# One norm for two, a rounding step without GpSimd, and sixteen gather places in a four-layer transformer kernel

## What is computed

```python
def _layernorm(x, axis=-1, eps=1e-05):
    return (x - mean(x)) / jnp.sqrt(var(x) + eps)

# third attention: it is called with _layernorm(x), and norms its input once more
def _L2_xattn_ref(hidden_states, cond, ln_w, ln_b, ...):
    ln_out = _ln(hidden_states, ln_w, ln_b)          # the second norm in a row
    # _fp8_linear_pertensor(ln_out, w, w_scale, in_scale), for q, k, v and qx:
    #   y = clip(ln_out / in_scale, -448, 448) -> bfloat16 -> float8_e4m3fn
    ...

# fourth feed-forward part: 64 experts, the best 8 for each token, 128 places an expert
def _L3_ffn_ref(hidden_states, router_weight, gate_up_proj, down_proj):
    topw, topi = jax.lax.top_k(softmax(x @ router_weight.T), 8)
    xe = x gathered by expert                        # (64, 128, 256)
    h = silu(g) * u                                  # g, u = xe @ gate_up_proj
    ye = h @ down_proj                               # (64, 128, 256)
    y = sum over the 8 experts of ye[its place] * weight

x = x + _L2_xattn_ref(_layernorm(x), ctx, ...)
...
x = x + _L3_ffn_ref(_layernorm(x), ...)
```

## Time and profile before

| | |
|---|---|
| Runs | 1892.12, 1887.36, 1890.64 us; median 1890.64 |
| Profiled execution | 1887.24 us, span of its instructions 1885.5 us |
| Mean granted TensorE clock | 0.871 of full speed |
| Busy (share of the span) | TensorE 1544.3 us (82%), VectorE 1120.1 (59%), ScalarE 813.7 (43%), GpSimd 777.2 (41%) |
| First norm to the end of the rounding stage | 868.2 to 921.8 us |
| Gathers and scatters of the sparse stage | 1678.6 to 1853.8 us |

### The profile page before, as it was taken

How to read it: one execution, slowest core, us unless ns; L and a number is a source line. 1 busy time by engine, 2 the same in 40 slices (tenths; PEclk the granted TensorE clock), 3 DMA queues, 4 the chain that set the end, 5 groups by cost and what they waited for, 6 DMA issues and landing times. The chain is left out here.

```text
span 1885.5 us, 25460 instructions
## 1 busy us (share of the span) xinstructions
PE 1544.3 (82%) x8600; PEld 982.3 (52%) x8600; DVE 1120.1 (59%) x2581; ACT 813.7 (43%) x1887; POOL 777.2 (41%) x1038
## 2 busy tenths in 40 slices
PE   6566659999797899994499999999699989837772
PEld 5322225656464455653266676666556565525551
DVE  5999971223674533426789999999622255463335
ACT  2898863110333211113488888888521112412221
POOL 1276641000200497800578777777310000026772
PEclk9666558999697999997699999999799988858886
DMA  2298871110504013111100000000111100146646
GB/s 76 59 180 180 177 153 44 34 42 17 179 2 163 34 56 120 56 45 46 45 1 1 2 1 1 1 2 1 43 29 39 37 24 1 69 177 214 244 140 239
DMA packets 174225, 140.13 MB, mean 74 GB/s; under 512 B 141793, under 2 KB 154721, under 8 KB 170386
## 3 DMA queue, kind: packets, MB, share of 16 engines
q1 hardware_dynamic: 165314, 114.89, 21.4%
q0 software_dynamic: 6416, 22.03, 3.5%
q10 hardware_dynamic: 2368, 1.61, 0.3%
HBM read 85.43 MB, written 19.50 MB: 56 GB/s over the span
## 5 line engine op out<-in xcount | busy, mean ns | idle before, releaser
L1817 POOL CAST l0m_pi<-l0m_pf 128x1024 bf16<-128x1024 int16 x128 | 133.2, 1040 | 111.1 <-ACT l0m_pf L1884 109.6
L1420 PE MATMUL l2x_pr<-l_w,l2x_xq 128*128 128x512 bf16 x576 | 141.4, 384 | 40.0 <-ACT credits L42 40.0
L350 PE MATMUL l1e_gu<-x_normT,l1e_w 128*128 128x512 f32 x384 | 171.6, 601 | 0.0
L1884 ACT ACTIVATE l0m_pf<-l0m_s,l0m_bias,l0x_sq 128x1024 int16<-128x1024 f32 x128 | 153.9, 1204 | 18.7 <-DVE l0m_bias L1915 12.3
L1911 DVE TENSOR_REDUCE l0m_mx<-l0m_s 128x1 f32<-128x1024 f32 x128 | 155.5, 1215 | 5.5 <-PE l0m_s L1826 5.2
L1555 DVE TENSOR_SCALAR l2x_raw<-l2x_raw,l2x_mv,l2x_rs 128x128 f32<-128x128 f32 x384 | 141.7, 429 | 1.6 <-POOL l2x_rs L1399 1.5
L1826 PE MATMUL l0m_s<-l0x_kT,l0x_qT 64*128 64x512 bf16 x256 | 69.0, 559 | 68.5 <-ACT l0m_pf L1884 65.7
L350 PE MATMUL l0e_gu<-x_normT,l0e_w 128*128 128x512 f32 x272 | 121.2, 600 | 0.0
L350 PEld LDWEIGHTS l1e_gu<-x_normT,l1e_w 128*128 128x128 f32 x384 | 74.0, 194 | 84.3 <-issue 83.3
L350 PE MATMUL l2e_gu<-x_normT,l2e_w 128*128 128x512 f32 x256 | 114.5, 602 | 0.0
L426 DVE TENSOR_TENSOR l1e_h<-l1e_sil,l1e_gu 128x512 f32<-128x512 f32 x40 | 27.5, 686 | 133.0 <-ACT l1e_sil L402 133.0
(11 more groups left out here) (516 smaller groups left out, 3562.8 us busy)
## 6 DMA issues: line engine op xcount, KB each, us to landing
l3m_w<-in_l_moe SPq DMA_DIRECT2D x16, 1280.0 KB, 6.4
l1e_w<-in_l_ffn SPq DMA_DIRECT2D x24, 384.0 KB, 3.0
l_rows<-zero_row SPq DMA_DIRECT2D x8, 1024.0 KB, 11.0
l_w<-l_rows SPq DMA_DIRECT2D x8, 1024.0 KB, 11.8
l0e_w<-in_l_ffn SPq DMA_DIRECT2D x17, 384.0 KB, 3.0
l2e_w<-in_l_ffn SPq DMA_DIRECT2D x16, 384.0 KB, 3.1
ctx_tok<-l_route SPq DMA_DIRECT2D x8, 512.0 KB
l2q_wps<-in_l_wp SPq DMA_DIRECT2D x16, 256.0 KB, 2.8
```

Source lines behind the costliest of these rows:

```text
L350: last = nc.tensor.matmul(gu[half][:, m, :], w[:, c % SW, (2 * k + m) * P:(2 * k + m + 1) * P], pg.xnT[:, k, cols(n)], start=(k == 0), sto ...
L1420: last = nc.tensor.matmul(flat(pr[t % 2][:]), src[:, k, tokens], pg.l2_w3[:, part, k, at:at + W], start=(k == 0 and part == 0), stop=(k == ...
L1817: nc.gpsimd.tensor_copy(pi[:, n % 8, :], pf[:, n % 4, :]).then_inc(s["rounded"], 1)
L1884: nc.scalar.activation(pf[:, n % 4, :], s_ps[n % 3][:], ACT.Exp, scale=sq[:, b, h:h + 1], bias=bias[:, n % 4:n % 4 + 1], accum_out=sm[:, b ...
```

## The change

Three things. The two norms in a row become one: the first norm is turned and takes the square root of var(1 + eps) + eps^2, which is what two norms in a row divide by; the block `l2xm` and the option `turn` go. The subtraction of the rounding stage moves from GpSimd to VectorE, as a fifth instruction of each job. The sparse stage has sixteen places for gathered rows, of which eight are filled ahead of the first scatter and two more behind each scatter until sixteen are reached; they lie in the buffer of the third layer's weights, which is no longer needed then, in place of a buffer of their own.

```diff
-def norm(pg, name, src, preload=None, turn=True):
+def norm(pg, name, src, preload=None, twice=False):
...
-                v.tensor_scalar(rs[:, 0, group], mv[:, group, 1], LN_EPS, None, ALU.add).then_inc(var_in, 1)
+                if twice:
+                    v.tensor_scalar(rs[:, 0, group], mv[:, group, 1], 1.0 + LN_EPS, LN_EPS ** 2, ALU.mult, ALU.add).then_inc(var_in, 1)
+                else:
+                    v.tensor_scalar(rs[:, 0, group], mv[:, group, 1], LN_EPS, None, ALU.add).then_inc(var_in, 1)
...
-            for i in range(PAIRS if turn else 0):
+            for i in range(PAIRS):
...
-    norm(pg, "l2xm", pg.xn)
...
-            @block.gpsimd
-            def _(pool):
-                for n, (k, j) in enumerate(jobs):
-                    pool.wait_ge(widened, n + 1)
-                    nc.gpsimd.tensor_tensor(xq[:, j, k, :], wide[:, n % 2], step[:, n % 2], ALU.subtract).then_inc(rounded, 1)
...
                     dve.wait_ge(divided, n + 1)
-                    if n >= 2:
-                        dve.wait_ge(rounded, n - 1)
                     ch.link(nc.vector.tensor_scalar(z[:, u], z[:, u], 448.0, -448.0, ALU.min, ALU.max))
                     widen(nc, ch, z[:, u], step[:, u], wide[:, u]).then_inc(widened, 1)
+                    dve.wait_ge(widened, n + 1)
+                    nc.vector.tensor_tensor(xq[:, j, k, :], wide[:, u], step[:, u], ALU.subtract).then_inc(rounded, 1)
+                dve.wait_ge(rounded, len(jobs))
...
-    GROUP, LOADS, AHEAD, NY = 4, 6, 6, 4
+    GROUP, LOADS, AHEAD, FIRST, NY = 4, 6, 16, 8, 4
...
-        xg = sb("xg", [P, AHEAD, ROW])
...
+        xg = spent[:, 0:AHEAD * ROW].rearrange("p (a n) -> p a n", n=ROW)
...
-            for e in range(AHEAD):
+            for e in range(FIRST):
                 gather(e)
             pool.wait_ge(pg.rows_zeroed, 16 * 8)
             for e in range(E):
                 scatter(e)
-                if e + AHEAD < E:
-                    gather(e + AHEAD)
+                for n in range(min(FIRST + 2 * e, e + AHEAD), min(FIRST + 2 * e + 2, e + AHEAD + 1)):
+                    if n < E:
+                        gather(n)
...
-                norm(pg, f"{name}n", pg.x, pre.load if pre else None, name != "l2x")
+                norm(pg, f"{name}n", pg.x, pre.load if pre else None, name == "l2x")
```

More of the change, by code:

```diff
@@ L195, in _ @@
         def _(pe):
-            if not turn:
-                return
             for i in range(PAIRS):
```

## The result

The changed kernel took 1862.9 us (median of 4 runs, 1858.9 to 1864.57), the kernel before on the same chip 1889.19 (4 runs, 1887.36 to 1892.12): ratio 0.9856, 95% interval 0.9833 to 0.9879. The profiled execution took 1861.34 us with a span of 1859.6, against 1885.5.

The account below looks back on a forecast made before the run. No single engine was taken to bound the kernel: VectorE stretched by GpSimd set rounding, GpSimd's issuing the sparse stage. Gains of 6.5 + 4.6 + 9.4 = 20.5 us gave 1870 us against the median, range 1863 to 1877.

Parts of the forecast that it names:

- Part 1: Third attention layer: one norm for two lets the rounding stage begin sooner; gain 6.47 us, bounds 6.2 to 6.6.
- Part 2: Rounding stage: subtraction on VectorE at 1.23 us, mask no longer stretched, 3.79 us a job; gain 4.64 us.
- rivals of a cheap and a dear subtraction: Rounding subtraction at 0.43 us: 6.4 us more gain, 1864, chance 0.03; at GpSimd's 2.23 us: part gives -3.4, no chance given.
- Part 3: Sparse stage: sixteen gather places remove GpSimd's middle waits; last scatter at 1844.4 against 1853.75, gain 9.4 us, bounds 0.6 to 11.3.
- stays at 1689.57, held by its own chain: Sparse stage start: two more gathers fill 2.5 of GpSimd's 3.52 us idle, but the first scatter comes no sooner.
- The tail's waits: Sparse stage end: the last 16 scatters, with no gather between, wait for experts at 1.63 us each; cost 1.9 us.
- no stall: Sparse stage: ScalarE's four output places suffice, four pairs of issues being 10.3 us against a landing of at most 6.5.
- gaps for ScalarE in the middle: Sparse stage: named as one sign that the forecast would be wrong; no size given.
- waits stay: Sparse stage rival: the middle waits remain, part 3 gives 0.6 us, total gain 11.7, time 1879; chance 0.10.
- slow clock: Sparse stage rival: TensorE granted 1.2 GHz throughout, 2.78 us an expert, 1890, no change; chance 0.04.
- late scatters: Sparse stage rival: landings above about 9.2 us hold up output places; at 13 us the time is 1908; chance 0.02.
- the sum: Whole kernel: 6.5 + 4.6 + 9.4 = 20.5 us gain, giving 1870.1 against the median.

Follow-up runs that it names:

- the repeated changed kernel: The changed kernel, unchanged, timed again with more executions beside the kernel before on one chip: 1863.41 us, ratio 0.9887.
- the run with small loads: The kernel before, six gather places, with ten weight loads of the sparse stage cut to 16 of 640 columns: 1878.77 us, one execution.
- The idle-time runs: Useless VectorE instructions after rounding; changed kernel with two, four, six, nine: 1862.7, 1872.95, 1870.14, 1873.33 us; kernel before with three, five: 1889.04, 1894.15 us.

## Why the prediction was right or wrong, by its steps

- **Part 1**: 6.46 us measured, 6.47 forecast. Right.
- **Part 2**: right in each step (mask 0.43, subtraction 1.23, clamps 3.78 apart where 3.79 was said). 4.73 us to the end of the last subtraction where 4.64 was said, 4.53 to the next stage's start, which is what the total gets. The rivals of a cheap and a dear subtraction are out.
- **Part 3**: mechanism right, size 10.2 in place of 9.4. The first scatter stood 10.18 us behind the first gather, not 10.94 as before. That is 0.8 us of luck: TensorE was granted 2.4 GHz sooner in this profile. The step "stays at 1689.57, held by its own chain" holds in the repeated changed kernel, with 10.89 us and a gap of 0.99 us, which is the 3.52 less 2.5 of the forecast. The tail's waits are 4.39 us in seven gaps, less 7 x 0.305, 2.3 us; 1.9 was forecast, and the repeated kernel has 1.4. An issue takes 1.281 us in place of 1.285, 0.5 us over the stage. One more thing was not in the forecast: with six places the stage takes 175.1 to 176.6 us over six profiles, with sixteen 164.5 to 166.2 over seven, so 10.2 is itself good to about 1 us. One step of this part was wrong and cost nothing: "no stall" for ScalarE at the output places. The kernel before had no such wait; in the changed one 51.2 us of the 67.5 lie in the middle of the stage, from 1690 to 1800 us, the longest 6.1 us. TensorE and ScalarE, no longer held by gathers, run ahead until the four places are full, and GpSimd's gaps stay at 0.3 us meanwhile. So the sign of being wrong that was named, gaps for ScalarE in the middle, came without the loss it was to announce. The middle waits of GpSimd vanished, and the run with small loads shows that they came from late landings. The rivals (waits stay, slow clock, late scatters) are out; scatters landed in at most 8.4 us, under the 9.2 from which it would have told, though nearer to it than the 6.5 of the earlier trace rows.
- **The step that failed is the sum**, "against the median: 1870.1" (20.5 us off a base of 1890.64). It took every stage outside the edits at its old length, and it took off from the median of three executions. The measured time is 7.2 us below 1870.1. Of these, 0.7 us is the edited stages, 21.2 in place of 20.5; 1.5 is the base, which fell to 1889.19 with a fourth execution; 4.7 is the stages outside the edits in the profiled pair, which the sum put at nothing; and 0.4 is left between the profiled pair, 25.9, and the medians, 26.3. That is the account by the first pair of profiles; the last point below says how far it holds for timed executions. Of the 4.7, 3.8 us, from 711.5 to 707.7 in the later stages, goes with TensorE's clock on work that nobody changed: 5.0 less in the fourth attention, 1.7 more in the third feed-forward part, and 0.5 less in the third attention, which was not traced further. The idle-time runs show that the length of the stretch ahead moves it. Another 0.9 lies ahead of all edits and is the execution's luck: those stages took 855.9 to 862.1 us in the profiles, from first aggregation to the third layer's first norm.
- **The base** was a high one. Later comparisons, of 23, 20 and 7 executions, had medians of 1886.3, 1885.71 and 1887.17. The forecast's 20.5 us against the steadier comparison, 0.9887 or 21.3 us (17.3 to 25.3), was close; the range of seven microseconds either way of 1870 was built for the edits' unknowns and had no room for two kernels' worth of spread and for stages that move by 4.
- **How much of the 3.8 us the timed runs have.** Little of it shows. The executions timed for each kernel of the experiments, and for the changed kernel, include its profiled one. In all five comparisons with a stretch of 41.6 us that one was faster than the median of the others, by 3.1 to 7.6 us; for the kernel before it was 3.0 slower. Without the profiled ones, the repeated changed kernel has a median of 1864.51 us against 1885.71, which is 21.2 less, just what the three edited stages give. The six such executions of both comparisons have 1864.5, and the 66 of the kernel before 1886.2: 21.7 less, on several chips. So what the first comparison's 26.3 has beyond 21.2 looks like the luck of four executions on either side, and so does its agreement with the profiled 25.9.

The single edits say the same. The rounding edit's profiled execution, with the later stages at 705.2 us, was the fastest of twelve (1878.17 to 1887.47), and its ratio gives 3 us of gain, not 4.5 + 6.4. The norm's was the fastest of six; its profile gives 6.5 + 3.6 and 3.3 more in the routing, 13.4 in all, and its ratio 9 (6.6 to 11.7).

What stays open: what decides whether the clock falls at a given place, and so why half a microsecond in the stretch (46.1 or 46.6) turns 708.0 into 714.1; and why the profiled executions of the changed kernel are faster than its others, of which only the total is on record.

## What to carry to other kernels

Where a queue of issues bounds a stage, look for its real gaps (idle time less the gap that every issue has) and give the thing that it waits for just enough depth: eight or ten places did here what sixteen did, and more depth left more scatters without a gather for the end, where the next limit (output places) showed. Moving work off an engine pays twice if the other engine stood still for it: eight instructions of 1.23 us were added and 4.5 us gained. And a change ahead of stages that run near TensorE's clock steps can move them by several microseconds either way: compare the stages one by one before crediting the edit, put idle time back as a control, and compare the profiled execution's time with the others of its kernel before carrying its stages over to them.

## What the runs showed of the hardware that was not expected

The granted clock of a stage repeated in the profiled executions where the idle stretch ahead had the same length (92.9 to 93.0 us of fourth attention in six profiles of one length, 97.9 to 98.0 in four of another) and changed with 2.5 us of idle time some 430 and 610 us ahead: the feed-forward part then took 184.0 us in place of 186.0, the fourth attention 97.2. The same work just ahead, with the same share busy, went with both levels: in the kernel before the clock fell to 1.2 GHz for 13.7 us in the middle of that attention, having been busy 8.38 of the 10 us before; in the changed kernel it stayed at 2.4 after the same 67 matmuls in 8.37 of 10 us. What decides it is not shown here.
